# Gated cross-attention and mixture-of-experts block on one Trainium2 core: bf16 thirds for the running maximum, a turned router product, and a rebuilt head

## Chip, core and metric

The kernel runs on one core of one Trainium2 chip. The metric is the device time of one launch in microseconds (us). The program is one launch; its output is 16 x 256 x 512 float32.

## What is computed

Sixteen sequences of 256 tokens, 512 wide. First a cell of the mLSTM kind with 8 heads of 64, with queries from the normed input and keys and values from a context; then a router over 16 experts with the best two taken, plus a shared expert that every token passes.

```python
# per sequence: q = layernorm(x), k = v = ctx
ig, fg   = gates of [q, k, v]                     # 8 rows each
cs       = cumsum(log_sigmoid(fg))
log_D    = where(tril, cs[:, None] - cs[None, :], -inf) + ig[None, :]
max_log_D = max(log_D, over keys)                 # one number per head and query
C        = (q k^T / 8) * exp(log_D - max_log_D)
h        = (C / (max(|sum C|, exp(-max_log_D)) + eps)) v
x        = x + tanh(g_xattn) * norm(h) * ln_scale
# then, on layernorm(x):
scores   = softmax(x @ router_w.T); top 2 of 16, renormed
y        = sum over the 2 experts of silu(x Wg) * (x Wu) @ Wd * weight
s        = silu(x @ shared_gate) * (x @ shared_up) @ shared_down
out      = x + tanh(g_ffn) * (y + s)
```

## The kernel before

Each sequence ("item") is two tiles of 128 tokens. A loop over steps t = -1 to 15, written out by hand once for every engine, interleaves four items: item t+1 at its front (load, norm, transposes, gates, the row of running maxima), item t in attention, item t-1 in the residual, second norm, router and shared expert, item t-2 in the rest of the shared expert and the placing of its tokens. The order in each engine's `step` is the order of its queue; events (semaphores) tie the engines together. After step 15 come a `drain`, the tables of the experts' tiles, 80 tiles of routed tokens through the experts, and a gather of the results. Only the steps and what stands ahead of them are touched by the change.

The parts that the prediction's steps touch:

- **The head.** SP loads x and context of items 0 and 1 (L348, L352) and then x of items 2 and 3. ACT issues eight small loads (L661) and then the three shared weight matrices of 1 MB each (L664) into the end of `base_out`. PE turns the gate and router rows (L878, L880) once all small loads are in, DVE copies them out of PSUM (L1199 to L1208). GpSimd (POOL) makes its constants in `other_constants` after the reciprocal root of item 0. In step -1 PE turns the context and the normed x of item 0 (L887), ACT copies them out (L669), PE forms the gates (L921), and DVE makes the rows: scan of the forget gates (L1251), keys (L1254), scan of the maxima (L1257), then `rows_end`.
- **The shared weights.** `split_shared` on POOL turns them, 128 x 6144 numbers, into a high fp32r part (L518) and a rest (L521), between step -1 and step 0 of POOL's queue. Both `shared` on PE and SP's loads beyond item 3 wait for it.
- **The spread of the maximum.** For each head, PE spreads the row of maxima over 128 partitions with `head_sel` (one row of ones per part) as the stationary operand. The row is held as two fp32r parts in rows 0 to 7 and 32 to 39, so the matmul contracts over 40 rows; it alternates with a bf16 matmul that adds the causal mask and contracts over 128 rows:

```python
for at, n in ((0, S), (S, P)):
    mm(MB[k][:, at:at + n], head_sel[0:FG + NH, h, :], max_parts[:, b.par, S - n:S],
       start=True, stop=False)
    last = mm(MB[k][:, at:at + P], identb[:, :], mask_b[:, :], start=False, stop=True)
```

- **The router.** With the tokens stationary and the router's weights moving (32 columns), 16 matmuls give the logits with tokens on partitions (L992); `keep_logits` on DVE adds the halves (L1356).

Of the kernel before, what the change touches and what calls it, by code (L numbers as in the profile page):

```python
# [78 lines left out]
def flamingo_kernel(nc, x, ctx_in, g_xattn, g_ffn, igate_w, igate_b, fgate_w, fgate_b, ln_scale,  # L79
# [8 lines left out]
    with ExitStack() as stack:  # L88
# [19 lines left out]
        head_sel = sb("head_sel", [P, NH, P], F32R)  # L108
# [6 lines left out]
        router_wT = sb("router_wT", [P, DC, 2 * E], F32R)  # L115
# [35 lines left out]
        max_parts = sb("max_parts", [FG + NH, 2, S], F32R)  # L151
# [19 lines left out]
        x2nT = sb("x2nT", [P, 2, DC, S], F32R)  # L171
        logits = sb("logits", [P, ST, E])
# [83 lines left out]
        row_step = event("row_step", 6)  # L256
# [21 lines left out]
        router_made = event("router_made")  # L278
        logits_made = event("logits_made")
# [49 lines left out]

        N_SMALL = 8  # L330
# [15 lines left out]
        def _(sp):  # L346
# [28 lines left out]
            with sp.Fori(0, (B - 4) // 2) as i:  # L375
                for u in range(2):
                    load_next(Item(i, 2 + u))
# [41 lines left out]
        def _(pool):  # L419
# [24 lines left out]
            def other_constants():  # L444
# [6 lines left out]
                const(g.memset(head_sel[:].bitcast(F32), 0.0))  # L451
                const(g.memset(v_aug[:], 1.0))
                const(g.memset(taken[:], 0.0))
                const(g.memset(max_parts[:].bitcast(F32), 0.0))
# [3 lines left out]
                for part in range(2):  # L458
                    select(head_sel[:], 1.0, ALU.not_equal, -FG * part, 1, [[-1, NH], [0, P]])
# [56 lines left out]
            def split_shared():  # L516
                pool.wait_ge(weights_in.sem, weights_in.upto(N_SHARED - 1))
                g.tensor_tensor(sh_flat[:, 0, :], sh_in, one[:, :].to_broadcast([P, 2 * EW]), ALU.mult  # L518
                                ).then_inc(shared_hi_in.sem, 1)
                pool.wait_ge(shared_hi_in.sem, shared_hi_in.upto(0))  # L520
                g.tensor_tensor(sh_flat[:, 1, :], sh_in, sh_flat[:, 0, :], ALU.subtract  # L521
                                ).then_inc(shared_in.sem, 1)

# [45 lines left out]

            stats(Item(0, 0))  # L570
            other_constants()
            step(Item(0, -1), attend=False, route=False, rest=False)
            split_shared()
# [72 lines left out]
        def _(act):  # L646
# [15 lines left out]
            for k, of in enumerate((shared_gate, shared_up, shared_down)):  # L662
                to = sh_in[:, k * DC * D:(k + 1) * DC * D].rearrange("p (c i) -> p c i", c=DC)
                act.dma_start(to, of.rearrange("(c p) i -> p c i", p=P)).then_inc(weights_in.sem, 16)  # L664
# [76 lines left out]
            def step(t, front=True, attend=True, route=True, rest=True):  # L741
# [5 lines left out]
                if attend:  # L747
                    head(A, 1)
                if rest:
                    shared(H, 2)  # L750
                if front:
                    turn_ctx(F, 0)
                if attend:
                    head(A, 2)
                    head(A, 3)
                if front:
# [3 lines left out]
                if front:  # L760
                    turn_x(F, 0)
                if rest:
                    keep(H, 2)
                if attend:
                    head(A, 4)
                    head(A, 5)
                if front:
                    turn_x(F, 1)
                if rest:
# [16 lines left out]
                if route:  # L786
                    shared(G, 0)
# [5 lines left out]
            def drain(G, H):  # L793
# [8 lines left out]
                turn(G, 1)  # L802
                top(G)
# [5 lines left out]
            step(Item(0, 0), route=False, rest=False)  # L809
# [61 lines left out]
        def _(pe):  # L871
# [11 lines left out]
            pe.wait_ge(wT_copied.sem, 6)  # L883
# [834 lines left out]
```

## Time and profile before

| | us |
|---|---|
| median of 3 runs (1299.69 to 1302.8) | 1300.96 |
| the profiled execution | 1299.23 |
| its span | 1297.7 |
| PE busy | 1111.2 (86%) |
| DVE busy | 749.3 (58%) |
| POOL busy | 478.2 (37%) |
| ACT busy | 387.6 (30%) |

PE, DVE, ACT and POOL are the matmul, vector, scalar and general engines; PEld is PE's load of the stationary operand, SP the engine that only issues loads. PE's busy time counts a pipelined matmul until its modelled end, so the distance from one start to the next is the better measure of what it costs. PEclk is the granted clock of PE as a share of 2.4 GHz. Idle time in square brackets is that of the engine just before the instruction, and the name behind it is what ended the wait.

### The profile page before, as it was taken

To read this page: it belongs to the slowest core of one execution; us is meant where nothing else is said; L and a number is where in the kernel's file an instruction comes from. 1 tells how busy PE (TensorE), PEld (TensorE's weight loads), DVE (VectorE), ACT (ScalarE), POOL (GpSimd) and SP (SyncE) were. 2 spreads that over 40 slices of the span, in tenths; PEclk is the share of its full clock that TensorE was granted. 3 is DMA by queue.
4 is the path that set the end of the run, shared out by engine and by line. 5 is a ranking of instruction groups with operands and counts; after the bars stand their busy time and mean duration, and the time that the engine had idled before them with its cause. 6 is when DMAs were issued, how large, how long until landed. Compare 5 with 4: busy or idle time off the path is not lost.

```text
span 1297.7 us, 23994 instructions
## 1 busy us (share of the span) xinstructions
PE 1111.2 (86%) x6643; PEld 912.9 (70%) x6644; DVE 749.3 (58%) x1940; ACT 387.6 (30%) x852; POOL 478.2 (37%) x368
## 2 busy tenths in 40 slices
PE   3099999999999999999999876999999999999000
PEld 2066888888888888888888764788888888887000
DVE  2835667676677677676667634544444444444365
ACT  1132344443343344343343101233232322322000
POOL 3700021222213220322122335366656657700675
PEclk9565899999999999999999978999999999999555
DMA  6010010111001110111000244555564645331798
GB/s 206 17 48 33 1 64 4 66 65 65 32 32 65 65 59 6 65 48 49 12 23 34 82 168 143 192 173 183 162 194 162 203 153 178 129 113 65 217 301 265
DMA packets 57849, 134.37 MB, mean 104 GB/s; under 512 B 7088, under 2 KB 7088, under 8 KB 57808
## 3 DMA queue, kind: packets, MB, share of 16 engines
q0 software_dynamic: 17472, 59.78, 14.1%
q1 hardware_dynamic: 26128, 48.51, 11.4%
q10 hardware_dynamic: 14208, 25.57, 5.5%
q8 instruction: 22, 0.36, 0.1%
q14 instruction: 19, 0.16, 0.0%
HBM read 83.23 MB, written 50.59 MB: 103 GB/s over the span
## 4 chain that ended last, share of the span: by engine, by line
PE 84%; DVE 6%; DMA 6%; issue 2%; ACT 1%; POOL 1%; DVEq 0%; POOLq 0%; ACTq 0%
PE bank L1141 18%; PE bank L1006 15%; PE bank L1159 9%; PE bank L1017 7%; PE bank L953 6%; PE bank L921 5%; PE bank L944 4%; DMA area<-routed_y,y_at 4%; PE bank L887 4%; PE bank L955 3%; PE bank L1129 3%; PE bank L992 2%; PE bank L966 2%; PE bank L968 2%; PE bank L965 2%
## 5 line engine op out<-in xcount | busy, mean ns | idle before, releaser
L1141 PE MATMUL bank<-w_ring,x2nT 128*128 x960 | 243.7, 403 | 7.1 <-DVE x2nT L1624 7.0
L1006 PE MATMUL bank<-x2nT,w_ring 128*128 128x256 f32 x1536 | 206.3, 293 | 3.2 <-DVE sh_act L1426 3.2
L1141 PEld LDWEIGHTS bank<-w_ring,x2nT 128*128 128x128 f32 x960 | 175.7, 190 | 46.8 <-issue 11.8
L1006 PEld LDWEIGHTS bank<-x2nT,w_ring 128*128 128x128 f32 x1536 | 195.6, 199 | 3.8 <-issue 3.6
L492 POOL DMA_INDIRECT routed_x<-x2n,slot_u x64 | 63.2, 988 | 250.8 <-DVE slot_u L1418 236.2
L1159 PE MATMUL bank<-w_ring,sh_actT 128*128 x480 | 125.4, 396 | 2.3 <-DVE sh_actT L1619 2.3
L513 POOL TENSOR_TENSOR sh_actT<-sh_act,sh_actT 128x256 fp32r<-128x256 f32 x64 | 46.8, 732 | 203.8 <-ACT sh_actT L732 203.8
L609 POOL TENSOR_TENSOR w_ring<-area,one 128x3072 fp32r<-128x3072 f32 x14 | 74.2, 5303 | 114.5 <-PE bank L1159 114.5
L1606 DVE SCALAR_TENSOR_TENSOR ctxT<-ctxT,bank 128x256 f32<-128x256 f32 x80 | 33.7, 421 | 142.5 <-ACT ctxT L834 142.5
L1159 PEld LDWEIGHTS bank<-w_ring,sh_actT 128*128 128x128 f32 x480 | 90.0, 188 | 24.3 <-issue 3.0
L1017 PE MATMUL bank<-w_ring,sh_actT 128*128 128x512 f32 x384 | 102.4, 418 | 2.3 <-DVE sh_act L1426 1.4
L1280 DVE SCALAR_TENSOR_TENSOR area<-bank,area 128x384 f32<-128x384 f32 x128 | 66.9, 553 | 58.1 <-PE bank L944 37.7
L632 POOL DMA_INDIRECT area<-routed_y,y_at x64 | 66.1, 1033 | 87.1 <-DMA routed_y<-cs_in 67.9
L612 POOL TENSOR_TENSOR w_ring<-area,w_ring 128x3072 fp32r<-128x3072 f32 x14 | 95.5, 6824 | 2.5 <-POOL w_ring L609 2.5
L953 PE MATMUL bank<-max_parts,head_sel 40*128 40x256 f32 (+1 forms) x256 | 93.9, 367 | 0.0
L834 ACT ACTIVATE ctxT<-bank 128x256 f32<-128x256 f32 x80 | 30.7, 384 | 202.5 <-PE bank L1141 202.5
L1017 PEld LDWEIGHTS bank<-w_ring,sh_actT 128*128 128x128 f32 x384 | 73.2, 198 | 18.6 <-DVE sh_act L1426 1.6
L1423 DVE SCALAR_TENSOR_TENSOR sh_act<-silu_t,bank 128x256 f32<-128x256 f32 x64 | 26.8, 419 | 83.6 <-ACT silu_t L727 83.6
L727 ACT ACTIVATE silu_t<-bank 128x256 f32<-128x256 f32 x64 | 24.5, 383 | 166.6 <-PE bank L1006 166.6
L840 ACT COPY cs_in<-bank 128x512 f32<-128x512 f32 x80 | 46.9, 586 | 87.8 <-PE bank L1159 87.8
L1617 DVE CAST sh_actT<-bank 128x256 fp32r<-128x256 f32 x80 | 34.0, 424 | 64.0 <-PE bank L1150 63.7
L953 PEld LDWEIGHTS bank<-max_parts,head_sel 40*128 40x128 f32 x256 | 49.4, 193 | 25.7 <-issue 11.8
(192 smaller groups left out, 2007.7 us busy)
## 6 DMA issues: line engine op xcount, KB each, us to landing
x2n<-routed_x SPq DMA_DIRECT2D x80, 256.0 KB, 2.7
routed_y<-cs_in ACTq DMA_DIRECT2D x80, 256.0 KB, 2.1
base_out<-in_x_dram SPq DMA_DIRECT2D x16, 512.0 KB, 4.8
cs_in<-in_ctx_dram SPq DMA_DIRECT2D x16, 512.0 KB, 3.5
area<-n_L_ffn_expert_gate_dram POOLq DMA_DIRECT2D x16, 512.0 KB, 4.1
area<-in_L_ffn_expert_up_dram POOLq DMA_DIRECT2D x16, 512.0 KB, 5.8
area<-n_L_ffn_expert_down_dram POOLq DMA_DIRECT2D x16, 512.0 KB, 7.1
out_dram<-area SPq DMA_DIRECT2D x32, 256.0 KB, 4.3
```

The lines of the kernel that those rows point to most:

```text
L492: pool.indirect_dma_start(out=routed_x, in_=x2n[:, b.par, j, :], in_offset=None, out_offset=bass.IndirectOffsetOnAxis(ap=slot_u[:, b.par, ...
L609: g.tensor_tensor(w_ring[:, k, 0, :], stage[k], one[:, :].to_broadcast([P, EW]), ALU.mult).then_inc(expert_hi_in.sem, 1)
L612: g.tensor_tensor(w_ring[:, k, 1, :], stage[k], w_ring[:, k, 0, :], ALU.subtract).then_inc(expert_in.sem, 1)
L632: pool.indirect_dma_start(out=y_in[k][:, c, :], in_=routed_y, out_offset=None, in_offset=bass.IndirectOffsetOnAxis(ap=y_at[:, k, c:c + 1], ...
L887: last = tr(TP[:, c * P:(c + 1) * P], src[:, c * P:(c + 1) * P], ident[:, :])
L921: last = mm(SM[0:FG + NH, 0:S], gate_wT[:, c, :], src, start=(c == 0), stop=(c == 2 * DC - 1))
L953: mm(MB[k][:, at:at + n], head_sel[0:FG + NH, h, :], max_parts[:, b.par, S - n:S], start=True, stop=False)
L1006: last = mm(GU[m][:, at:at + S], w[:, w_part, c, m * P:(m + 1) * P], x2nT[:, x_part, c, :], start=(c + p == 0), stop=(c == DC - 1 and p == 2))
L1017: last = mm(FF[:, :], sh_actT[:, x_part, m, j * P:(j + 1) * P], sh_down[:, w_part, m, :], start=(m + p == 0), stop=(m == SC - 1 and p == 2))
L1141: last = mm(bank[2 + t.par][:, :], xtT[:, x_part, t.par, c * P:(c + 1) * P], w_gu[:, bass.ds(slot, 1), w_part, c, :].rearrange("p a i -> p ...
L1159: last = mm(bank[5 + t.par][:, :], act_aT[:, x_part, t.par, c * P:(c + 1) * P], w_dn[:, bass.ds(slot, 1), w_part, c, :].rearrange("p a i - ...
L1280: v.scalar_tensor_tensor(cmat[:, k, :], QK[k][:, 0:TRI], QK_SCALE, decay[:, k, :], ALU.mult, ALU.mult).then_inc(c_made.sem, 1)
```

## The change

Four things are done. The row of maxima is held in three bf16 parts (rows 0, 32 and 64), and `spread` contracts over 96 rows, all in bf16; DVE makes the parts with two more instructions. The router's weights are padded to 128 columns and become the stationary operand, so that 8 matmuls with 256 moving columns give the logits with experts on partitions; ACT copies 32 rows of them out, and two small matmuls per item turn them back and add their halves. The first loads and constants are reordered: SP loads x and context of item 0 alone, waits for both, then loads item 1, x of item 2 and the shared weights; POOL makes most constants first and those of `head_sel` after the first norm; DVE takes the statistics of item 0 ahead of the weight copies. The shared weights are split in six pieces within step 0, the high part on ACT and the rest on DVE.

```diff
-        max_parts = sb("max_parts", [FG + NH, 2, S], F32R)
+        max_rest = sb("max_rest", [FG + NH, S])[FG:, :]
+        max_parts = sb("max_parts", [P, 2, S], BF16)
@@ sync
-            for n in range(2):
-                load_x(Item(0, n))
-                load_ctx(Item(0, n))
-            for n in range(2, 4):
-                sp.wait_ge(x_in[n % 2].sem, x_in[n % 2].upto(0))
-                load_x(Item(0, n))
-            sp.wait_ge(shared_in.sem, shared_in.upto(0))
+            load_x(Item(0, 0))
+            load_ctx(Item(0, 0))
+            sp.wait_ge(x_in[0].sem, x_in[0].upto(0))
+            sp.wait_ge(c_in[0].sem, c_in[0].upto(0))
+            load_x(Item(0, 1))
+            load_ctx(Item(0, 1))
+            load_x(Item(0, 2))
+            for k, of in enumerate((shared_gate, shared_up, shared_down)):
+                to = sh_in[:, k * DC * D:(k + 1) * DC * D].rearrange("p (c i) -> p c i", c=DC)
+                sp.dma_start(to, of.rearrange("(c p) i -> p c i", p=P)).then_inc(weights_in.sem, 16)
+            sp.wait_ge(x_in[1].sem, x_in[1].upto(0))
+            load_x(Item(0, 3))
+            for u in range(2):
+                load_next(Item(0, 2 + u))
+            sp.wait_ge(shared_in.sem, shared_in.upto(SHARED_PIECES - 1))
@@ gpsimd
-            stats(Item(0, 0))
             other_constants()
+            stats(Item(0, 0))
+            head_constants()
             step(Item(0, -1), attend=False, route=False, rest=False)
-            split_shared()
@@ scalar
+            def router(b):
+                act.wait_ge(router_made.sem, router_made.upto(b.n))
+                s.copy(logit_row[:, :], SM[0:2 * E, 0:S]).then_inc(logit_row_made.sem, 1)
+            def piece(k):
+                act.wait_ge(weights_in.sem, weights_in.upto(N_SHARED - 1))
+                at = slice(k * SHARED_PIECE, (k + 1) * SHARED_PIECE)
+                s.copy(sh_flat[:, 0, at], sh_in[:, at]).then_inc(shared_hi_in.sem, 1)
@@ tensor
-                    mm(MB[k][:, at:at + n], head_sel[0:FG + NH, h, :], max_parts[:, b.par, S - n:S],
+                    mm(MB[k][:, at:at + n], head_sel[0:3 * FG, h, :], max_parts[0:3 * FG, b.par, S - n:S],
-                for j in range(ST):
-                    for c in range(DC):
-                        for part in range(2):
-                            last = mm(SM[:, j * 2 * E:(j + 1) * 2 * E], x2nT[:, part, c, j * P:(j + 1) * P],
-                                      router_wT[:, c, :], start=(c + part == 0), stop=(c == DC - 1 and part == 1))
-                last.then_inc(router_made.sem, 1)
+                for c in range(DC):
+                    for part in range(2):
+                        last = mm(SM[:, 0:S], router_wT[:, c, :], x2nT[:, part, c, :],
+                                  start=(c + part == 0), stop=(c == DC - 1 and part == 1))
+                last.then_inc(router_made.sem, 1)
+            def logits_pe(b):
+                pe.wait_ge(wT_copied.sem, 9)
+                pe.wait_ge(logit_row_made.sem, logit_row_made.upto(b.n))
+                apart(pe)
+                for j in range(ST):
+                    last = mm(SM[:, j * E:(j + 1) * E], logit_row[:, j * P:(j + 1) * P], pair_ident[:, :],
+                              start=True, stop=True)
+                last.then_inc(logits_turned.sem, 1)
@@ vector
-                v.tensor_tensor(max_parts[FG:, b.par, :], max_row[:, :], max_parts[0:NH, b.par, :], ALU.subtract
+                v.tensor_tensor(max_rest[:, :], max_row[:, :], max_parts[0:NH, b.par, :], ALU.subtract
                                 ).then_inc(row_step.sem, 1)
+                v.tensor_copy(max_parts[FG:FG + NH, b.par, :], max_rest[:, :]).then_inc(row_step.sem, 1)
+                v.tensor_tensor(max_parts[2 * FG:2 * FG + NH, b.par, :], max_rest[:, :],
+                                max_parts[FG:FG + NH, b.par, :], ALU.subtract).then_inc(row_step.sem, 1)
+            def piece(k):
+                dve.wait_ge(shared_hi_in.sem, shared_hi_in.upto(k))
+                at = slice(k * SHARED_PIECE, (k + 1) * SHARED_PIECE)
+                v.tensor_tensor(sh_flat[:, 1, at], sh_in[:, at], sh_flat[:, 0, at], ALU.subtract
+                                ).then_inc(shared_in.sem, 1)
```

In step 0 ACT has its pieces 0 to 5 after `head` 1, `turn_ctx` 0, `head` 3, `turn_x` 0, `head` 5 and `turn_x` 1; DVE has them after `head` 1, `head` 3, `out_pair` 0, `norm_front` 1, `head` 5 and `out_pair` 1. In every step with a router, ACT's copy stands ahead of `shared(G, 0)`, and `logits_pe` on PE after `pv` 7 and ahead of `shared(G, 1)`. DVE's weight copies gain a memset of `router_wT` (128 x 512) and the making of `pair_ident`.

## Rows read from the trace of the kernel before

**Rows 1.** Busy time per stretch: start:end, length, PE, PEld, DVE, ACT, POOL, PEclk, DMA, GB/s.
```profile
63.00:101.60 38.60, 34.16 (x148) 24.62 (x148) 13.35 (x38) 13.04 (x28) 0.69 (x1) 0.59 0.16 54
149.30:694.20 544.90, 544.90 (x3826) 454.81 (x3826) 379.46 (x1136) 215.72 (x495) 128.88 (x155) 0.99 0.13 45
```
**Rows 2.** Timeline of the head, first loads to gates: start, us, engine, line, operation.
```profile
4.79 0.32 ACTq L661 DMA_DIRECT2D gate_bias<-in_L_xattn_fgate_b_dram  x1
5.71 4.70 SPq L348 DMA_DIRECT2D base_out<-in_x_dram  x2
...
13.63 0.20 ACT L666 ACTIVATE tanh_g<-g_col 128x2 f32<-128x2 f32 x1 [4.55 <-DMA gate_bias<-in_L_xattn_fgate_b_dram]
...
16.63 1.11 PE L887 MATMUL bank<-ident,cs_in 128*128 128x128 f32 x4 [1.03 <-DVE gate_wT L1208]
...
19.89 4.29 DVE L1235 TENSOR_SCALAR xn<-base_out,ln_mv,ln_rstd 128x512 f32<-128x512 f32 x1 [0.92 <-POOL ln_rstd L499]
...
28.49 3.42 PE L921 MATMUL bank<-area,gate_wT 128*40 128x256 f32 x8 [0.68 <-ACT area L669]
```
**Rows 3.** Timeline of the head, rows of item 0 beside POOL's split of the shared weights.
```profile
37.41 10.42 POOL L518 TENSOR_TENSOR w_ring<-base_out,one 128x6144 fp32r<-128x6144 f32 x1
37.62 10.50 DVE L1254 TENSOR_TENSOR key_max<-gates,f_row 8x256 f32<-8x256 f32 x1
...
48.15 13.48 DVE L1257 TENSOR_TENSOR_SCAN max_row<-key_max 8x256 f32<-8x256 f32 x1
...
63.00 1.67 PE L944 MATMUL bank<-area,ctxT 64*128 64x256 f32 x8
```
**Rows 4.** Timeline of DVE in later steps: a row scan and a row subtraction.
```profile
96.42 0.68 DVE L1251 TENSOR_TENSOR_SCAN f_row<-one,f_row 8x256 f32<-8x256 f32 x1
...
226.40 0.41 DVE L1265 TENSOR_TENSOR max_parts<-max_row,max_parts 8x256 fp32r<-8x256 f32 x1
```
**Rows 5.** Timeline of PE: the four matmuls of one head's spread at full clock.
```profile
238.16 0.38 PE L953 MATMUL bank<-max_parts,head_sel 40*128 40x256 f32 x1
238.47 0.23 PE L955 MATMUL bank<-mask_b,identb 128*128 128x128 bf16 x1
238.63 0.32 PE L953 MATMUL bank<-max_parts,head_sel 40*128 40x128 f32 x1
238.89 0.23 PE L955 MATMUL bank<-mask_b,identb 128*128 128x128 bf16 x1
```
**Rows 6.** Timeline of PE: two of the four bf16 matmuls that rank tokens.
```profile
259.08 0.17 PE L979 MATMUL bank<-taken,ones_b 128*128 128x16 bf16 x1
259.10 0.17 PE L980 MATMUL bank<-chosen,before_b 128*128 128x16 bf16 x1
```
**Rows 7.** The chain that ended last: start, us, what.
```profile
264.79 1.89 PE bank L992 x16
266.68 2.97 PE bank L1006 x24
...
576.87 0.85 PE bank L944 x8
577.73 0.59 PE bank L887 x4
...
581.18 0.44 PE bank L887 x4
```
**Rows 8.** Timeline of PE in step 0: the first matmuls of two heads' spreads.
```profile
77.57 0.58 PE L953 MATMUL bank<-max_parts,head_sel 40*128 40x256 f32 x1
...
78.92 0.58 PE L953 MATMUL bank<-max_parts,head_sel 40*128 40x256 f32 x1
```
**Rows 9.** Timeline of PE in step 1: the first router.
```profile
136.97 3.27 PE L992 MATMUL bank<-router_wT,x2nT 128*128 128x32 f32 x16 [2.62 <-DVE x2nT L1432]
```
**Rows 10.** Timeline of ACT in one step: its copies of the turned x.
```profile
246.13 0.58 ACT L669 COPY area<-bank 128x512 f32<-128x512 f32 x1
...
249.34 0.58 ACT L669 COPY area<-bank 128x512 f32<-128x512 f32 x1 [0.71 <-PE bank L887]
```

More of the change, by code:

```diff
@@ L457, in other_constants, with head_constants @@
                 select(mask_b[:], MASK, ALU.is_ge, 0, -1, [[1, P]])
-                for part in range(2):
+            def head_constants():
+                pool.wait_ge(xn_made.sem, xn_made.upto(0))
+                const(g.memset(head_sel[:], 0.0))
+                for part in range(3):
                     select(head_sel[:], 1.0, ALU.not_equal, -FG * part, 1, [[-1, NH], [0, P]])
@@ L748, in step @@
                     head(A, 1)
+                if split:
+                    piece(0)
                 if rest:
@@ L752, in step @@
                     turn_ctx(F, 0)
+                if split:
+                    piece(1)
                 if attend:
@@ L755, in step @@
                     head(A, 3)
+                if split:
+                    piece(2)
                 if front:
@@ L761, in step @@
                     turn_x(F, 0)
+                if split:
+                    piece(3)
                 if rest:
@@ L802, in drain @@
                 turn(G, 1)
+                router(G)
                 top(G)
@@ L808, in _ @@
             step(Item(0, -1), attend=False, route=False, rest=False)
-            step(Item(0, 0), route=False, rest=False)
+            step(Item(0, 0), route=False, rest=False, split=True)
             step(Item(0, 1), rest=False)
@@ L1454, in count_rows, with step @@
                 v.tensor_copy(pad_tab[:, :], pad_f[0:1, :]).then_inc(pads_made.sem, 1)
-            def step(t, ahead=True, front=True, attend=True, route=True, rest=True):
+            def piece(k):
[3 more added lines that the diff above has]
+                                ).then_inc(shared_in.sem, 1)
+            def step(t, ahead=True, front=True, attend=True, route=True, rest=True, split=False):
                 N, F, A, G, H = t + 2, t + 1, t, t + -1, t + -2
@@ L1462, in step @@
                     head(A, 1)
+                if split:
+                    piece(0)
                 if front:
@@ L1471, in step @@
                     head(A, 3)
+                if split:
+                    piece(1)
                 if route:
@@ L1487, in step @@
                     head(A, 5)
+                if split:
+                    piece(4)
                 if route:
@@ L1491, in step @@
                     out_pair(A, 1)
+                if split:
+                    piece(5)
                 if front:
@@ L1557, in drain @@
                 shared(G, 1)
-            stats(Item(0, 0))
             step(Item(0, -1), attend=False, route=False, rest=False)
-            step(Item(0, 0), route=False, rest=False)
+            step(Item(0, 0), route=False, rest=False, split=True)
             step(Item(0, 1), rest=False)
```

99 lines of the change are left out of this document (55 added, 44 removed).

## The prediction
> **What bounds the kernel now.** I read the span by stages first. From 149.3 to 694.2 us, steps 2 to 14, PE is busy without a gap: 544.9 of 544.9 us at a clock of 0.99, while DVE has 379 and ACT 216 [rows 1]. That is 13 steps of 41.9 us, and whatever leaves PE's queue there leaves the time, as long as no other engine's chain becomes later than PE. Ahead of that stands a head in which PE waits. The timeline of the head shows two holds. The last small load is issued at 4.79 us, but the work that needs it starts at 13.63 [rows 2]; it shared the DMA engines with two items' inputs and three 1 MB matrices. Later DVE's subtraction of 8 x 256 numbers takes 10.50 us and a scan 13.48, exactly while POOL splits the shared weights, against 0.41 and 0.68 elsewhere [rows 3, 4]. In the timeline PE's first scores start at 63.00 only when that is over. The first norm is held in the same way by POOL's constants: 4.29 us for a 128 x 512 tile [rows 2]. What comes after the steps (drain, experts, gather) isn't touched; I carry it over as it is.
>
> **The head.** (a) Without the split beside them, subtraction, scan and the key row take 0.45, 0.71 and 0.45 us with the hand-over, so scores of item 0 would start at 37.62 + 1.6 + 0.15 = 39.4 instead of 63.0: **23.6 us** [rows 3, 4]. The two new row instructions (0.41 each, [rows 4]) and ACT's part run while PE does its scores (1.67, [rows 3]), so they cost nothing here; should they show, it is 0.8 us. (b) The small loads: x of item 0 had landed at 5.71 with everything beside it [rows 2]. With only item 0 ahead of them they can land between about 6 (just after their issue ends at 5.1) and 13.6 (no gain); I take 8, as they are small and issued first, and the 3 MB of weights now queue behind item 1 on SP: **5.6 us**. (c) DVE's weight copies have a memset of 128 x 512 and one more dependent step in front of the event PE waits for: 0.6 us lost. The statistics of item 0 come before, under the wait for the loads, and need x only. (d) From the first context transpose (16.63) to the gates (28.49) it is 11.9 us [rows 2]. Uncontended it is four links of transpose and copy, each 1.1 + 0.6 + hand-over, 1.8 us, so 7.2: **4.6 us**. POOL's `head_constants` then run behind the second norm, under the gates; they are due only when the rows of item 0 are made, some 8 us later. Together the head gives 23.6 + 5.6 - 0.6 + 4.6 = **33 us**; bounds 25 (small loads hardly earlier, constants in the way) and 35.
>
> **The spread.** At full clock the four matmuls start at 238.16, .47, .63, .89 and the next head follows 0.16 later: 0.31 + 0.16 + 0.26 + 0.16 = 0.89 us for a head [rows 5]. The columns that stream are 256 + 3 x 128, and the stream of 256-column fp32r matmuls shows 2.97/24 = 0.124 us each [rows 7], so columns alone need about 0.12 + 3 x 0.055 = 0.28 us. The rest, 0.6 us, is four times 0.15, and there are four changes between a 40-row and a 128-row contraction. 0.15 us is also what four transposes cost more after the 64-row scores than elsewhere, 0.59 against 0.44 [rows 7]. So I read the 0.15 as the price of a change of the array's row shape. A change of type with the rows unchanged is cheap: the ranks' bf16 matmuls stand 0.03 us apart between fp32 neighbours, load of the stationary operand included [rows 6]. With 96 rows both matmuls fill the same row shape, so I take 0.28 us for a head. The trace has no 96-row matmul; the bounds are 0.28 (all hidden) and about 0.67 (a load of 0.10 us exposed in front of each, the mask matmul's 0.16 less its 0.055 of columns: 0.28 + 4 x 0.10). Eight heads now cost 6.9 us in a step (the last mask matmul of a pair is partly hidden), afterwards 2.3 plus 0.35 for entering after the 64-row scores and for leaving to fp32: 4.3 us saved. The Trainium skill (TensorE: Matmul & The Clock Gate, "Back-to-back issue gap") gives 81 ns for a 128-column matmul in a stream of loads and matmuls; by it, as an estimate, a head would cost 0.36 us and the whole time would be 9 us longer than my sum. The ranks' 0.03 us speaks against so high a floor.
>
> DVE gets two row instructions more, 0.8 us a step, at the place where it makes the rows; it has 29 us of work in a step of 42 [rows 1], and what is queued behind them (`shared` of item t-1) waits for PE there, so I cost them at nothing. If that cover goes, it is 0.8 us in each of 14 steps.
>
> **The router.** 16 matmuls in 1.89 us [rows 7] become 8 with 256 columns at 0.124, 1.0: 0.9 saved. The two turning matmuls are fp32 over 32 rows, with a change of shape in and out. Nothing like it is in the trace: below, four passes at 0.03 make 0.1, above, four at 0.1 with 0.15 in and out make 0.7; I take 0.5, nearer to the upper one since fp32 passes here cost 0.11 (0.44/4, [rows 7]). ACT's copy stands ahead of its tanh and waits for the router, but its tanh needs `shared(G, 0)`, 2.97 us later, which covers the 0.4 and a table load. `logits_pe` stands behind `shared(G, 0)` and two `pv`, so its wait is over when PE comes to it. Net 0.4 saved.
>
> **The sum of the steps.** Steps 2 to 14: 13 x 4.7 = **61 us**. Step 15, the same spreads: **4.7**. In steps 0 and 1 PE runs mostly at half clock (0.59, [rows 1]); a head costs 78.92 - 77.57 = 1.35 us there [rows 8] and would cost 0.55: 0.8 saved. In step 0, six heads give 4.9 us; for heads 6 and 7 PE then waits for the rows in any case. The pieces add about 1.05 us each on ACT (twice the 0.58 of 512 columns, [rows 10], less its fixed part) and 1.2 on DVE (four times the 256-column 0.41, [rows 4], less its fixed part; up to 1.6), 6 to 10 us on engines that have 13 us of work in 38.6 [rows 1]. In order, counted through the queues with these prices, they put the second norm of the front at about 14.4 us of step 0 and PE's need for it at 14.9, so they fit, barely; uncovered they cost up to 7. I take 4.7 saved. In step 1: 6.5, with 0.5 more for the router (3.27 there, [rows 9]) included and its wait of 2.62 kept. The drain: router shorter by about 1 us, logits later by as much: 0.
>
> 33 + 4.7 + 6.5 + 61 + 4.7 = **110 us**. Against the profiled execution's own 1299.2 (span 1297.7) that is 1189; the median of the runs is 1.7 above it, so I say **1190**.
>
> **Rivals.**
> *Exposed loads.* The new bf16 pair doesn't pipeline and a head costs 0.67. Then a step gives 1.6 us instead of 4.7, 14 times, and a little less in steps 0 and 1: 110 - 46 = 64, time **1236**. For it: the sum of load and stream fits the present 0.16 of the mask matmul as well. Against it: the ranks' 0.03 us [rows 6] and the 0.124 of fp32r on the same rows [rows 7]. The Trainium skill (same page, Part 3, "The mechanism") states that a load overlaps a running matmul only where the row groups differ; that rule gives this rival's time. These rows contradict it. Chance 0.10.
> *A chain of ACT or DVE takes over.* The tightest one: between the two copies of the turned x, ACT has the copy, a cast and two heads' exponentials, and 0.71 us of slack in 3.2 [rows 10], so the second copy is out 3.1 us after the first began. PE gets from the end of the first transposes to the gates over two spreads (0.6), scores (0.95 with the change of shape), transposes (0.5) and two `pv` (some 1.35) in 3.4 instead of 4.5 us. A second one: the first `pv` comes 1.1 us earlier after the scores. If these lose 1.5 us in each of 14 steps, it is **1211**. Chance 0.20.
> *The clock, the other side.* Such waits in PE's stream could bring the granted clock down to 1.2 GHz inside the steps, as in step 0. The router took 3.27 us at half clock against 1.89 [rows 7, 9], 1.7 times; on a step of 36.9 that is 26 us more. The place is the wait before the gates; from more than four whole steps of the 14 at half clock the gain is gone, and with six the time is **1345**. Against it: 0.99 over 13 steps [rows 1]. Chance 0.02.
> *The clock rises sooner.* PE's pause in the head shrinks and steps 0 and 1 run partly at full clock: 15 us, **1174**. Chance 0.12.
> *The hold isn't the split.* If DVE's 24 us had another cause, (a) is lost: **1213**. The coincidence in [rows 3] speaks against it. Chance 0.03.
>
> **How the numbers follow.** My forecast has 0.53; no more than 0.13 may lie above with the exposed loads and the slow clock. The range takes in the forecast with its bounds (pieces uncovered +7, head -2 to +8, turning matmuls -6 to +3), the early clock and the chain: 1173 to 1221. A measurement of this kernel can tell 0.2%, 2.6 us, from no change. Faster by more than that: 0.97, within it 0.01, slower 0.02 (the clock).
>
> **What would show it.** Scores of item 0 near 30 us. In the steady steps a distance of 36.8 us from router to router, PE still without a gap, and the matmuls of a spread 0.06 to 0.12 us apart; 0.15 to 0.20 would be the exposed loads. Idle PE ahead of L921 or the first `pv` would be the chain. The small loads in before 9 us. DVE's row scan at 0.7 us in the head. I am wrong if the steps shrink by under 3 us or over 6, or if step 0 is as long as before.

## The result, and the profile after

The changed kernel takes 1203.32 us (median of 4 runs, 1201.28 to 1205.39), the kernel before on the same chip 1301.88: a ratio of 0.924 [0.922, 0.927]. The forecast was 1190, in a range of 1173 to 1221. The profiled execution took 1202.77 us, its span 1201.3, so the two spans differ by 96.4 us; the prediction's terms add to 110.

The page after: its busy times, the queue q14, one of the two on which instructions are fetched (packets, MB, share), and the head of the chain that ended last:

```profile
span 1201.3 us, 23893 instructions
PE 1027.4 (86%) x6579; PEld 872.3 (73%) x6580; DVE 739.1 (62%) x1980; ACT 392.1 (33%) x874; POOL 456.3 (38%) x367
...
q14 instruction: 39, 0.32, 0.1%
...
PE 82%; DVE 6%; DMA 5%; issue 4%; ACT 1%; POOL 0%; DVEq 0%; ACTq 0%; POOLq 0%
```

PE's share is the 86% that it was; what went is 84 us of its busy time and some waits. The stages answer to [rows 1] (columns as there): step 0, step 1, steps 2 to 14 but for their last 3 us and, last, one undisturbed step.

```profile
32.50:63.50 31.00, 24.46 (x147) 19.52 (x147) 21.34 (x47) 18.32 (x34) 0.69 (x1) 0.72 0.11 35
63.50:98.60 35.10, 30.83 (x216) 26.86 (x217) 25.18 (x68) 14.36 (x32) 3.79 (x5) 0.83 0.10 31
98.60:600.80 502.20, 490.07 (x3747) 429.09 (x3747) 385.39 (x1157) 215.08 (x507) 126.06 (x152) 0.97 0.13 48
252.80:289.70 36.90, 36.90 (x291) 32.38 (x290) 29.84 (x90) 16.50 (x39) 9.93 (x13) 1.00 0.16 57
```

The undisturbed step is as forecast: PE busy for all of it, at a clock of 1.00. Over steps 2 to 14 together that is not so: PE is idle for 12.1 us of the stretch, and the clock stands at 0.97. Before, it had no gap there.

To see where, I took the start of each step in both traces (the matmul with which PE turns the maxima of item t onto partitions) and the distance to the next. Before, it is 41.55 us in ten of steps 2 to 14 and 43.1 in steps 7, 10 and 13; after, it is 36.98 in nine and 43.30, 42.93, 43.43 and 42.86 in steps 5, 7, 9 and 11. That gives this ledger, in us of the two spans:

| stage | before | after | gain | forecast |
|---|---|---|---|---|
| up to step 0 | 62.85 | 32.13 | 30.7 | 33 |
| steps 0 and 1 | 86.3 | 66.4 | 19.9 | 11.2 |
| steps 2 to 14 | 544.8 | 505.3 | 39.5 | 61 |
| step 15 to the end | 603.7 | 597.4 | 6.3 | 4.7 |

The third line splits further: 13 x (41.55 - 36.98) = 59.4 us are gained, the 4.7 us of the three longer steps before are gained too, and four steps give back 6.3, 5.95, 6.45 and 5.9, 24.6 us in all.

What the long steps hold is plain in the timeline of DVE at the start of step 5 (start, us, engine, line, operation, idle before it and its releaser):

```profile
211.63 0.16 DVE L1449 TENSOR_TENSOR all_w<-all_w,gap_exp 128x2 f32 x1
215.52 1.29 DVE L1364 BATCH_NORM_STATS2 h_stat<-area 128x6 f32<-128x512 f32 x2 [3.73 <-issue]
```

L1449 is the last instruction of one step and L1364 the first of the next. DVE stands for 3.73 us between them and waits for nothing that this view shows. PE runs dry behind it, and its clock then falls; the timeline of PE, the chain, and the windows from there on:

```profile
218.17 0.43 PE L996 MATMUL bank<-area 128*128 128x65 f32 x2 [3.07 <-DVE area L1332]
```
```profile
220.23 1.58 PE bank L975 x8
...
222.86 4.25 PE bank L1045 x24
```
```profile
216.00:222.00 6.00, 3.83 (x21) 3.32 (x22) 4.78 (x12) 1.36 (x4) 0.69 (x1) 0.75 0.00 1
222.00:228.00 6.00, 6.00 (x40) 5.90 (x39) 3.66 (x10) 1.39 (x3) 0.00 (x0) 0.68 0.00 0
228.00:234.00 6.00, 6.00 (x41) 4.28 (x40) 5.66 (x23) 2.71 (x9) 2.11 (x3) 1.00 0.00 0
```

The chain's eight scores take 1.58 us and 24 matmuls of L1045 4.25, against 0.85 and 2.87 in other steps: half clock, 1.2 GHz, for part of 12 us, at a clock of 0.75 and 0.68. So such a step pays about 3 us of PE's wait and 3 of clock. The table of waits (total us, count, longest) counts it; four of the five and of the six are these, and 4.1 us of PE's lie in step 0:

```profile
PE bank L996 <- DVE area L1332: 16.2, 5, 4.1
...
DVE h_stat L1364 <- issue: 15.1, 6, 3.9
```

The four places are the four times that DVE's program jumps back in its loop (`dve.Fori`, five laps of two steps, steps 3 to 12). PE, ACT and POOL have the same loop and jump too, but no such gap stands in PE's timeline on its own account. And the queue q14 carried 39 packets where it carried 19 before: five more, of 8 KB each, for each of the four jumps. The times of these packets in the trace go further. DVE's branch stands at 211.72 us; a packet starts at 213.4, within the gap, and the next at 216.0, half a us after its end; it is so at the other three jumps too (1.5 to 1.9 us behind the branch, and 0.3 to 0.5 behind the gap). In the kernel before no packet at all goes over q14 between 255.4 and 613.7 us, while DVE is in its loop. Theory A, with which the experiments begin, is that DVE has to fetch its loop again at each jump back, and that the instructions that the change adds brought this about. Rivals: the two new row instructions, the router's copy or the pieces make a chain late (B), or something in the memory traffic of these steps does (C).

### The profile page after: what moved, and what is told of

The parts are those of the page before. It is cut to its first block, busy times and chain, and to the rows that moved or that the text cites. A ratio compares the mean times of both kernels' runs of the same rounds, so it can differ in the third digit from the quotient of the medians.

```text
span 1201.3 us, 23893 instructions
## 1 busy us (share of the span) xinstructions
PE 1027.4 (86%) x6579; PEld 872.3 (73%) x6580; DVE 739.1 (62%) x1980; ACT 392.1 (33%) x874; POOL 456.3 (38%) x367
## 3 DMA queue, kind: packets, MB, share of 16 engines
q0 software_dynamic: 17472, 59.78, 14.9%
## 4 chain that ended last, share of the span: by engine, by line
PE 82%; DVE 6%; DMA 5%; issue 4%; ACT 1%; POOL 0%; DVEq 0%; ACTq 0%; POOLq 0%
PE bank L1182 19%; PE bank L1045 15%; PE bank L1200 9%; PE bank L1056 8%; PE bank L952 5%; DMA area<-routed_y,y_at 5%; PE bank L975 4%; PE bank L918 4%; PE bank L1170 3%; PE bank L996 2%; PE bank L997 2%; PE bank L999 2%; PE bank L984 2%; PE bank L1022 2%; PE bank L1191 1%
## 5 line engine op out<-in xcount | busy, mean ns | idle before, releaser
L1045 PE MATMUL bank<-x2nT,w_ring 128*128 128x256 f32 x1536 | 206.9, 293 | 3.2 <-DVE sh_act L1478 3.2
L1045 PEld LDWEIGHTS bank<-x2nT,w_ring 128*128 128x128 f32 x1536 | 197.0, 200 | 4.2 <-issue 3.6
L511 POOL DMA_INDIRECT routed_x<-x2n,slot_u x64 | 63.9, 998 | 222.8 <-DVE slot_u L1470 198.8
L643 POOL DMA_INDIRECT area<-routed_y,y_at x64 | 66.4, 1038 | 86.7 <-DMA routed_y<-cs_in 67.5
L1686 DVE CAST sh_actT<-bank 128x256 fp32r<-128x256 f32 x80 | 34.0, 425 | 63.8 <-PE bank L1191 63.5
L739 ACT ACTIVATE silu_t<-bank 128x256 f32<-128x256 f32 x64 | 24.6, 384 | 134.0 <-PE bank L1045 134.0
L723 ACT ACTIVATE area<-bank,key_log 128x256 f32<-128x256 f32 x128 | 61.4, 480 | 15.5 <-DVE area L1332 11.2
L975 PE MATMUL bank<-area,ctxT 64*128 64x256 f32 (+1 forms) x512 | 65.2, 369 | 0.0
L996 PE MATMUL bank<-area 128*128 128x65 f32 x256 | 51.0, 282 | 16.2 <-DVE area L1332 16.2
```

Source lines behind the costliest of these rows:

```text
L511: pool.indirect_dma_start(out=routed_x, in_=x2n[:, b.par, j, :], in_offset=None, out_offset=bass.IndirectOffsetOnAxis(ap=slot_u[:, b.par, ...
L643: pool.indirect_dma_start(out=y_in[k][:, c, :], in_=routed_y, out_offset=None, in_offset=bass.IndirectOffsetOnAxis(ap=y_at[:, k, c:c + 1], ...
L723: s.activation(decay[:, k, 0:S], MB[k][:, 0:S], ACT.Exp, bias=key_log[:, b.par, 0, h:h + 1], scale=-1.0)
L975: last = mm(QK[k][:, at:at + n], ctxT[half, b.par, q, frm:frm + P], xnT[half, b.par, q, S - n:S], start=True, stop=True)
L996: mm(HO[:, r:r + VW], cmat[:, k, 0:P], v_aug[:, b.par, 0, h, :], start=True, stop=True)
L1045: last = mm(GU[m][:, at:at + S], w[:, w_part, c, m * P:(m + 1) * P], x2nT[:, x_part, c, :], start=(c + p == 0), stop=(c == DC - 1 and p == 2))
```

## The experiments

"Written out" is one edit, in all kernels with u_ in their names: DVE's loop becomes a Python loop, the instructions unrolled.

```diff
-            with dve.Fori(0, (B - 6) // 2) as i:
+            for i in range((B - 6) // 2):
                 step(Item(i, 3))
                 step(Item(i, 4))
```

**The changed kernel, written out (u_after).** 

> The changed kernel with DVE's loop over steps 3 to 12 written out in full (five times two steps, no branch), nothing else. In the changed kernel DVE stands still for about 3.5 us ahead of the first instruction of steps 5, 7, 9 and 11, just behind the branch back of its loop, and these four steps take 43.1 us instead of 36.98. Theory A (the branch back makes DVE fetch instructions again, because loop and place no longer fit what it holds): the four stalls are gone, time 1203 - 25 = 1178. Theory B (POOL's scatters or the clock hold DVE in every second step, whatever the code is): the stalls stay, time within 3 us of 1203.

Measured: 1172.95 us (1171.80 to 1173.83), 0.902 [0.900, 0.905] of before, 30 us under the changed kernel. All thirteen steps 2 to 14 are 36.98 us. Windows of steps 0, 1 and 2 to 14, and the wait of `h_stat`:

```profile
32.50:60.00 27.50, 20.98 (x146) 17.22 (x145) 21.51 (x48) 18.39 (x34) 0.69 (x1) 0.81 0.11 39
60.00:92.50 32.50, 28.23 (x217) 24.23 (x216) 25.19 (x68) 14.35 (x32) 3.79 (x5) 0.92 0.10 34
92.50:573.20 480.70, 480.70 (x3773) 421.39 (x3772) 385.19 (x1162) 214.40 (x507) 129.97 (x155) 1.00 0.14 51
```
```profile
DVE h_stat L1364 <- issue: 0.3, 1, 0.3
```

PE is busy for 480.70 of 480.70 us with the same work on every engine. B and C are out: every chain and every transfer of data is still there, only the jumps are gone. Of the 29.4 us between the two spans, 24.6 are the four jumps and 6.2 are steps 0 and 1, at a higher clock here (see the last section); what follows step 14 is 1.3 longer.

**The kernel before, written out (u_before).** 

> The kernel before with DVE's loop written out in full. It has only 0.4 us in front of each of its steps 5, 7, 9, 11 on DVE, and PE has no gap there, so both theories expect no change: 1298 to 1302. It is the base for the parts by themselves.

Measured: 1300.53, 1.0005 [0.999, 1.002]. The loop cost nothing before: no gap at its four jumps then.

**Where the loop lies.** Both kernels, loop kept, with increments of a semaphore (`apart(dve)`) that do nothing else ahead of it:

```diff
 pad_before (before):  ahead of dve.wait_ge(wT_made.sem, 1)
+            for _ in range(19):
+                apart(dve)
 pad_after (after), pad110_after (after):  ahead of stats(Item(0, 0))
+            for _ in range(120):      # pad110_after: range(110)
+                apart(dve)
```

pad_before: 

> The kernel before with 19 semaphore increments on DVE ahead of the wait for the turned weights, under a wait of 15 us; the loop's length is as before (372), its last instruction lies as far along as in the changed kernel. A1 (place): four stalls of some 3.5 us appear, in a stream of PE with more slack, 4 to 6 us each: 1318 to 1326. A2 (length): no change, 1301.

Measured: 1309.04, 1.008 [1.005, 1.011]. Steps 5, 7, 9 and 11 are now 45.7, 44.1, 44.4 and 44.1 us in a kernel that has neither the new spread nor the new router. DVE's timeline, its waits and the page's queue:

```profile
279.73 1.29 DVE L1314 BATCH_NORM_STATS2 h_stat<-area 128x6 f32<-128x512 f32 x2 [3.65 <-issue]
```
```profile
DVE h_stat L1314 <- issue: 15.0, 6, 3.9
```
```profile
q14 instruction: 39, 0.32, 0.1%
```

The stall and the 20 packets are there: 19 instructions in front of the loop are enough. The expectation had 1318 to 1326, a good deal too much. PE's row at the first of them says why, with the clock behind it:

```profile
282.38 0.43 PE L965 MATMUL bank<-area 128*128 128x65 f32 x2 [0.86 <-DVE area L1282]
```
```profile
279.00:285.00 6.00, 5.13 (x29) 4.12 (x29) 4.99 (x12) 2.32 (x6) 0.69 (x1) 0.82 0.01 1
285.00:291.00 6.00, 6.00 (x35) 5.60 (x36) 3.63 (x10) 0.59 (x1) 0.00 (x0) 0.61 0.00 0
```

The same stall, 3.65 us on DVE, comes out on PE as 0.86 instead of 3.07, presumably because the longer spreads of before give PE more work in the meantime; no run parts that. The clock falls all the same (0.82 and 0.61). The four steps lose 12.1 us together, about 3 each where the changed kernel loses 6.15. One of the longer steps of before is gone in return (1.55) and steps 0 and 1 are 2.4 shorter in this execution, while the head is 0.8 longer and the part from step 15 on 1.6: 10.5 us between the two spans. The medians lie 8.8 apart.

pad_after: 

> The changed kernel with 120 semaphore increments on DVE ahead of everything else, so that the loop keeps its length and its branch, but lies 120 instructions later. Theory A1 (what counts is where the loop lies against blocks of the instruction memory): the four stalls go, about 1180, plus up to 3 us for the increments, which mostly run while DVE waits for the first load. Theory A2 (what counts is the length of the loop, 375 instructions against 372 before): the stalls stay, 1203 to 1206.

Measured: 1213.88 (1206.95 to 1218.74), 0.935 [0.931, 0.939]. A miss: the four long steps stay (43.9 to 44.5 us), and so do the packets.

```profile
DVE h_stat L1366 <- issue: 19.7, 6, 4.9
```

The stalls are even longer, 4.8 to 4.9 us, with two packets within each gap instead of one. Not every shift removes them, then. I counted the instructions of DVE's compiled program, waits and register instructions included, ahead of the loop and in it: before 323 and 372 (no stall), pad_before 342 and 372 (stall), after 339 and 375 (stall), pad_after 459 and 375 (stall). The traces confirm the first of each pair; a lap takes 376 or 379 instructions in them, four more than the count. A packet of 8 KB holds some 128 instructions, of 64 bytes: in u_after, where nothing jumps, one packet comes in each of steps 5 to 13, and DVE runs 128 to 130 instructions from one to the next. If DVE keeps three such blocks, a loop of 376 or 379 fits into 384 only if it starts within the first 9 or 6 instructions of a block (12 or 9 by the first count). Where in a block the count begins isn't known, but one block further on must do about as well as 323 does: 451, less a few for the longer loop. 110 increments put it at 449, 120 at 459.

pad110_after: 

> The changed kernel with 110 increments on DVE ahead of everything instead of 120. So far the four stalls are absent only with the loop's start at instruction 323 and 372 long, and present at 339 and 459 (375 long) and 342 (372 long); each brings some 20 fetch packets of 8 KB (128 instructions) in all, 5 a time. Theory A3: DVE holds blocks of 128 instructions and reaches back over three of them, so the loop must start within the first 9 to 12 instructions of a block; before it did, and 110 puts the changed loop at the same place less 2 (126 = 128 - 2 further): no stalls, 1203 - 25 + 3 for the increments = 1181. If blocks are of another size or more is held: stalls as in the changed kernel, 1206 to 1213.

Measured: 1177.80 us (1172.31 to 1186.29), 0.904 [0.900, 0.908]. 110 useless instructions make the changed kernel 25 us faster than it is; with ten more it takes 36 us longer again, of which 29.1 are the four long steps of pad_after. Steps 2 to 14 are 36.98 but for one of 37.02.

```profile
DVE h_stat L1366 <- issue: 2.0, 5, 0.5
```
```profile
q14 instruction: 20, 0.16, 0.0%
```

The packets go back to 20, and none goes over q14 between 198.8 and 515.6 us, while DVE is in its loop. So the loop, its length and its branch are those of the changed kernel, and its place alone decides: that the place of the loop is the cause is shown. That DVE keeps three blocks of 128 is a reading that fits the five positions. Six blocks of 64 instructions would fit them equally well, so the size isn't settled; two blocks of 256 don't, since a count that lets 323 and 449 pass and stops 339 and 342 would let 459 pass too. Nor is it explained why a jump brings five packets, where a loop that starts late in a block touches four.

The Trainium skill (Runtime: NRT & Kernel Launch, "Instruction fetch mechanics") says that a taken branch whose target lies outside a window of two pages of 256 instructions forces a fetch. The kind of stall is the one seen here, 3.5 to 4.9 us each, but the positions that stall aren't those of its page size.

**The loop written out on PE, ACT, DVE and POOL (u4_after).** 

> The changed kernel with the loop over steps 3 to 12 written out on PE, ACT, DVE and POOL. The trace shows no wait at the branch of the other three, so: no change from DVE's alone, 1171 to 1175; faster only if some engine's loop registers cost in PE's stream, which has no gap.

Measured: 1180.65 (1173.99 to 1187.06), 0.906 [0.901, 0.911], steps of 36.98. Two of the four runs lie in the range expected (1174.0 and 1174.4), two at 1187.0 and 1187.1; in the profiled one, 1186.96, steps 0 and 1 take 10 us more than in u_after (see the last section). Nothing is gained on the other three engines; only DVE's loop stalled.

**The spread alone (u_spread)**, on the kernel before, written out: three bf16 parts over 96 rows, old router, old head. 

> On the kernel before with DVE's loop written out (1300.5): the bf16 spread over 96 rows alone. The prediction's terms: 4.3 us in each of 13 steps and in step 15 (60), 4.9 and 5 in steps 0 and 1 at half clock, 70 in all, and the three dips of the clock (1.55 us each, in steps 6, 9 and 12 of the kernel before) may go with it: 1226 to 1231. Theory of the row shape: matmuls of a spread 0.06 to 0.12 us apart. If loads stay exposed: 1275.

Measured: 1218.20 (1212.69 to 1223.28), 0.936 [0.931, 0.940]. Steps 2 to 14 are 37.14 us, 4.41 less than 41.55, the forecast's 4.3. Steps 0 and 1 gain 14.9 us (86.55 to 71.7) where 9.9 were expected: their clock is 0.67 and 0.67 instead of 0.59 and 0.66, behind a head as long as before (63.2 us to step 0 against 63.5). The three steps of 43.1 are gone. So the time is 8 us below the range expected, though the step itself is as forecast. The timeline of PE in the changed kernel, to hold against [rows 5]:

```profile
608.34 0.28 PE L984 MATMUL bank<-max_parts,head_sel 96*128 96x256 bf16 x1
608.46 0.22 PE L986 MATMUL bank<-mask_b,identb 128*128 128x128 bf16 x1
608.51 0.22 PE L984 MATMUL bank<-max_parts,head_sel 96*128 96x128 bf16 x1
608.57 0.22 PE L986 MATMUL bank<-mask_b,identb 128*128 128x128 bf16 x1
608.63 0.27 PE L984 MATMUL bank<-max_parts,head_sel 96*128 96x256 bf16 x1
```

A head costs 608.63 - 608.34 = 0.29 us where it cost 0.89.

**Shape or type.** The change alters both. Two kernels alter one. u_rows40 is the changed kernel, written out, with two of the three bf16 parts over 40 rows (it leaves the third part of the maxima out); u_rows96 is the kernel before, written out, with fp32r parts over 96 rows, rows 40 to 95 zero.

```diff
 u_rows40
-  head_sel[0:3 * FG, h, :], max_parts[0:3 * FG, b.par, S - n:S]
+  head_sel[0:FG + NH, h, :], max_parts[0:FG + NH, b.par, S - n:S]
 u_rows96
-  head_sel[0:FG + NH, h, :], max_parts[:, b.par, S - n:S]
+  head_sel[0:3 * FG, h, :], max_parts[0:3 * FG, b.par, S - n:S]
```

u_rows40: 

> The changed kernel with DVE's loop written out (1173, a step 36.98 us, a head's spread 0.285 us), but the spread's bf16 product contracts over rows 0 to 39, two of the three parts; the third part of the maximum is left out. All bf16, and the row shape changes four times a head. If the change of row shape is the price (theory of the prediction): a head costs 0.28 + 4 x 0.1 to 0.15, 0.7 to 0.9 us, a step 3.3 to 4.9 us more: 1219 to 1242. If it was the fp32r operand or the change of type: no change, 1173.

u_rows96: 

> The kernel before with DVE's loop written out (1300.5, a step 41.55), but the fp32r product contracts over 96 rows, of which those past the second part are zero. The type changes four times a head, the row shape doesn't. If the row shape is the price: a head falls from 0.89 to 0.3 to 0.45 us, a step to 37.0 to 38.3, time 1220 to 1250. If the type is: 1300.

Measured: u_rows40 1227.78, 0.945 [0.942, 0.947], steps of 39.94; u_rows96 1237.74, 0.952 [0.950, 0.953], steps of 38.28. The timeline of PE, first u_rows40, then u_rows96:

```profile
169.85 0.28 PE L984 MATMUL bank<-max_parts,head_sel 40*128 40x256 bf16 x1
170.07 0.23 PE L986 MATMUL bank<-mask_b,identb 128*128 128x128 bf16 x1
170.23 0.23 PE L984 MATMUL bank<-max_parts,head_sel 40*128 40x128 bf16 x1
170.39 0.23 PE L986 MATMUL bank<-mask_b,identb 128*128 128x128 bf16 x1
```
```profile
220.41 0.36 PE L953 MATMUL bank<-max_parts,head_sel 96*128 96x256 f32 x1
...
220.84 0.36 PE L953 MATMUL bank<-max_parts,head_sel 96*128 96x256 f32 x1
```

In u_rows40 a head is one distance of 0.22 us and three of 0.16, 0.70; in u_rows96 it is 220.84 - 220.41 = 0.43 here and 0.44 as the median of 40 heads. The medians of all four kernels:

| us a head | 40 rows | 96 rows |
|---|---|---|
| fp32r parts | 0.89 | 0.44 |
| bf16 parts | 0.70 | 0.29 |

The rows make up 0.45 of the head with fp32r parts and 0.41 with bf16 parts, a quarter of which is 0.10 to 0.11 us for each change of the row shape. The type makes 0.15 to 0.19. Whether that is the price of alternating two types or of the fp32r operand itself isn't separated, as no kernel here holds all four matmuls in fp32r. The steps agree: 96 rows alone bring 3.27 of the 4.41 us, and going back to 40 rows in bf16 costs 2.96. The Trainium skill (TensorEngine Tiling (Array Packing), "Key Properties") says that a change of tiling mode drains the engine. It gives no price; if going from 40 to 128 rows is such a change, these runs give one.

**The router alone (u_router)**, on the kernel before, written out. 

> On the same base (1300.5): the turned router alone. By the prediction 0.9 us less for 8 instead of 16 matmuls and 0.5 for turning the logits back, 0.4 a step: 13 x 0.4 + 1 = 6 us, 1294 to 1296. From the changed kernel's rows (1.15 instead of 1.89, then 0.54): 0.2 a step, 1297 to 1298.

Measured: 1286.99 us (1286.64 to 1291.95), 0.991 [0.988, 0.994]. A miss: more is gained than expected, and not where. A step of 2 to 14 gains 0.16 us (41.55 to 41.39). The chain of the changed kernel, against the 1.89 of [rows 7], says why:

```profile
163.64 1.15 PE bank L1022 x8
...
168.94 0.54 PE bank L1031 x4
```

The router's 8 matmuls save 0.74 and the turning costs 0.54. Of the 15.7 us between the spans of the two profiled executions, 4.9 lie in steps 0 and 1 (86.55 to 81.7), 2.1 in steps 2 to 14 and 9.3 after the start of step 15, of which 5 come ahead of the first expert (108.0 to 103.0); the head loses 0.5. The windows that begin 50 us after the start of step 15, first u_before, then u_router:

```profile
744.86:754.86 10.00, 8.50 (x39) 7.32 (x38) 2.90 (x8) 1.17 (x2) 1.29 (x2) 0.67 0.01 2
```
```profile
738.44:748.44 10.00, 8.49 (x44) 6.76 (x42) 2.85 (x7) 1.38 (x3) 2.21 (x3) 0.92 0.06 26
```

PE is busy for as long, but gets 44 matmuls done instead of 39, at a clock of 0.92 instead of 0.67. The drain is shorter by clock, then, not by work. It doesn't take the new router: in u_rows96, which has the old one, the first expert comes 102.5 us after the start of step 15, as early as here. Why the clock comes back there earlier stays open, as do the 4 us in the experts' part, where no instruction differs.

**The hold by POOL's split (u_poolsplit)**: the changed kernel, written out, with `split_shared` back on POOL ahead of step 0 and no pieces.

```diff
             step(Item(0, -1), attend=False, route=False, rest=False)
+            split_shared()
             step(Item(0, 0), route=False, rest=False)
```

> The changed kernel with DVE's loop written out (1173), but the shared weights split by POOL in two instructions between steps -1 and 0, as before the change, and no pieces on ACT and DVE. If POOL's split is what holds DVE (term a): the row subtraction and scan of item 0 take over 10 us again, the first scores come 23 us later, step 0 gets the pieces' price back (0 to 4): 1192 to 1197. If DVE was held by something else: 1169 to 1174.

Measured: 1198.30 (1194.95 to 1207.18), 0.921 [0.918, 0.923], 25.4 us above u_after and 1.3 above the range. Timeline of POOL and DVE:

```profile
30.03 10.42 POOL L537 TENSOR_TENSOR w_ring<-base_out,one 128x6144 fp32r<-128x6144 f32 x1
30.24 10.49 DVE L1310 TENSOR_TENSOR key_max<-gates,f_row 8x256 f32<-8x256 f32 x1
...
40.76 13.48 DVE L1313 TENSOR_TENSOR_SCAN max_row<-key_max 8x256 f32<-8x256 f32 x1
```

In the changed kernel the same two instructions take 1.08 and 0.68. Step 0 starts at 55.5 against 32.3 in u_after: 23.1 us. The split was the hold.

**The order of the first loads (u_loads_old)**: the changed kernel, written out, with SP's order of before and the three matrices issued by ACT again.

```diff
-            load_x(Item(0, 0))
-            load_ctx(Item(0, 0))
-            sp.wait_ge(x_in[0].sem, x_in[0].upto(0))
-            ...
+            for n in range(2):
+                load_x(Item(0, n))
+                load_ctx(Item(0, n))
```

> The changed kernel with DVE's loop written out (1173), but the first loads in the old order: both items at once on SP, shared weights behind the small loads on ACT. By term b the work on the small loads starts at 13 to 14 us instead of 9.0, first scores 4 to 5 us later: 1177 to 1178. If the new order is worth nothing: 1173.

Measured: 1177.46 (1175.83 to 1184.91), 0.907 [0.903, 0.911]. PE's first work waits until 13.98 for the last small load, and step 0 starts at 36.8, 4.5 us later than in u_after:

```profile
13.98 1.43 PE L906 MATMUL bank<-ident,x2n 16*128 16x16 f32 x12 [13.98 <-DMA gate_bias<-in_L_xattn_fgate_b_dram]
```

## Why the prediction was right, and where it wasn't

**The head (33 forecast, 30.7 measured)** held in all its terms, (a) and (b) being 1.5 and about 1 us too large. Timeline of the changed kernel, to hold against [rows 2, 3]:

```profile
9.01 0.20 ACT L674 ACTIVATE tanh_g<-g_col 128x2 f32<-128x2 f32 x1 [3.15 <-DMA gate_bias<-in_L_xattn_fgate_b_dram]
...
12.67 1.11 PE L918 MATMUL bank<-ident,cs_in 128*128 128x128 f32 x4 [1.70 <-DVE gate_wT L1269]
...
19.93 3.63 PE L952 MATMUL bank<-area,gate_wT 128*40 128x256 f32 x8 [0.68 <-ACT area L677]
...
29.79 1.08 DVE L1301 TENSOR_TENSOR key_max<-gates,f_row 8x256 f32<-8x256 f32 x1
30.90 0.68 DVE L1304 TENSOR_TENSOR_SCAN max_row<-key_max 8x256 f32<-8x256 f32 x1
```

(a) 23.6 for the hold: u_poolsplit gives 23.1. From gates to scores 22.1 are gained here, as the key row takes 1.08 and starts later after the gates. (b) and (c) together 5.0: the first context transpose comes at 12.67 instead of 16.63, 4.0; the small loads were in by 9.0, not 8, and u_loads_old gives 4.5 for (b). (d) 4.6: from there to the gates it is 7.26 us against 11.86, 4.6.

**The spread.** Right in size and in cause: 0.29 us a head for 0.28, 4.41 us a step for 4.3. The reading of the 0.15 was partly off. Four changes of shape carry 0.41 to 0.45 of the 0.6, and the type, a change of which the prediction called cheap by the ranks' rows, has 0.15 to 0.19. Both fell to the same edit, so the sum didn't notice; that is luck. The rival of exposed loads (0.67 a head) is refuted by the row at 608.46: 0.05 us from the mask matmul to the next of 96 rows.

**Step 15 and after** gave 6.3, forecast 4.7. The agreement is in part luck. The parts don't add up there: behind the start of step 15 the spread alone gives 2.0 us, the router alone 9.2, 96 rows in fp32r 5.6 and all of the change 6.3, since the clock of the drain, which I had at 0, changes with each of them.

**The router.** Net 0.4 a step forecast, 0.16 measured: the turning matmuls were in their bracket (0.54 for 0.5), but 8 matmuls take 1.15 instead of 1.0, at 0.144 each and not 0.124.

**Steps 0 and 1** gave 19.9 instead of 11.2. The counts were right, the clock wasn't: 0.72 and 0.83 where it was 0.59 and 0.66. This is the rival in which the clock rises sooner, half fulfilled in its size. Its reason, the shorter pause of PE in the head, isn't borne out: u_spread gains 14.9 of these us behind the old head, and u_poolsplit, whose step 0 starts at 55.5 us, and pad110_after, whose starts at 35.2, take the same 30.8 and 39.3. The pieces cost little, if anything. PE waits 1.63 us for the turn of x in step 0 (L918 at 44.89), which I had as barely covered, but only where its clock is high; u_poolsplit without pieces and pad110_after with them need the same 30.8 us for step 0.

**Steps 2 to 14: the step that failed** is the sentence that DVE's two row instructions are costed "at nothing", with 29 us of work in a step of 42 as cover. It named the cover for their run time, which holds, and had no term for what instructions do by their place. The change put 16 more instructions ahead of DVE's loop and 3 into it (pad_before shows that 19 ahead of it are enough; pad110_after that the 3 within it are no hindrance). Each of the four jumps back then cost 6.15 us, 24.6 in all, of a forecast gain of 61. Without them the steps gave 64.1 (13 x 4.57, and 4.7 for the longer steps of before, which the forecast hadn't either). That DVE's work itself is covered is shown by u_after and pad110_after, which run the same instructions on it without a loss.

So the number came as near as it did by luck, by errors against each other: 24.6 lost in jumps against 8.7 won by the clock in steps 0 and 1 and 4.7 by the three longer steps of before, which were clock too (see the last section). The rival of a late chain gave 1211, nearer to the 1203 than the forecast, but its mechanism is refuted: no wait on ACT or DVE takes PE's place in the 480.70 us of u_after. The rival that the hold isn't the split is refuted by u_poolsplit. The slow clock was there in places (0.68 for 6 us), on the scale of a jump, not of a step.

The version that beats both kernels is the changed one with DVE's loop written out, 1172.95 us.

## What to carry to other kernels

An instruction added can cost far more than its run time: by moving a loop of its engine to where each jump back stalls (here 6.15 us a jump). Look for idle time "<- issue" at the loop's first instruction and for packets of the instruction queue in proportion to the laps, and write the loop out, or shift it, if you find them. In a stream of small matmuls, count the changes of row shape: at 0.10 to 0.11 us each they can outweigh the columns. A large POOL instruction stretched small DVE ones beside it to its own length (10.42 and 10.49 us), so do such work on another engine, or in pieces beside work that doesn't wait.

## What the runs showed of the hardware that I had not expected

- A jump back on DVE stalls it for 3.5 to 4.9 us or not at all, by where the loop starts: 449 instructions ahead, no stall, 459, stall (375 in the loop). Whether the loops of other engines would stall at other positions wasn't tried.
- One stall of 3.7 us costs 6.15 where PE has 3.1 us of wait from it and about 3 where it has 0.9: the fall of the clock, to 1.2 GHz for several us afterwards, is half or more of the price.
- The kernel before has three steps of 43.1 us, 126.2 apart, in which PE is never idle. They are dips of the clock: from 365 to 371 us PEclk is 0.68 and then 0.76, at full busy time of PE, and four transposes take 1.11 us and, behind the dip, 0.60 (timeline of PE):

```profile
367.43 1.11 PE L887 MATMUL bank<-ident,cs_in 128*128 128x128 f32 x4
...
371.72 0.60 PE L887 MATMUL bank<-ident,xn 128*128 128x128 f32 x4
```

- Such dips are gone in the kernels with bf16 parts or with 96 rows. Why the clock falls there without a wait stays open.
- Steps 0 and 1 take different times at equal work: 27.5 and 32.5 us in u_after, 31.0 and 35.1 in the changed kernel, 30.8 and 39.3 in pad110_after and u4_after. Some 10 us also part the runs of one kernel (u_spread: 1223.3 and 1223.2, 1212.7 and 1213.2; u4_after: 1187.0 and 1187.1, 1174.4 and 1174.0). What sets the course stays open. The windows of steps 0 and 1 of pad110_after have the matmuls of those of u_after, but a lower clock:

```profile
35.30:66.10 30.80, 25.96 (x148) 21.32 (x149) 21.57 (x49) 18.62 (x34) 0.69 (x1) 0.67 0.11 35
66.10:105.40 39.30, 35.78 (x218) 30.97 (x219) 24.69 (x68) 14.51 (x33) 3.79 (x5) 0.70 0.08 28
```
